# Two transformer layers on one core: the wait for the end of a GpSimd call at every third call instead of every second, and the engines' order chosen anew

## The reference

```
x = x + 0.5 * moe_swiglu(ln(x))          # f = 0
x = x + rwkv_time_mixing(ln(x))          # f = 1: a scan along the sequence
x = x + 0.5 * moe_swiglu(ln(x))          # f = 2, same weights as f = 0
x = x + 0.5 * moe_silu(ln(x))            # f = 3
x = x + retention(ln(x))                 # f = 4: 16 heads of 8, decay mask, group norm
x = x + 0.5 * moe_silu(ln(x))            # f = 5, same weights as f = 3
```

## Time and profile before

| what | value |
|---|---|
| median of 3 runs | 724.55 us (722.36 to 731.54) |
| profiled execution, its own time | 730.31 us |
| its span | 728.4 us |
| mean granted TensorE clock | 0.94 |
| busy: TensorE, VectorE, ScalarE, GpSimd | 606.1, 386.8, 344.1, 399.4 us |

### The profile page before, as it was taken

One profiled execution on the slowest core, in us unless ns is written; L12 is line 12 of the kernel. 1 busy time (PEld: TensorE's weight loads), 2 busy tenths in 40 slices (PEclk: granted clock), 3 DMA queues, 4 the chain that ended last, 5 costly groups with the idle time before them and its releaser, 6 DMA issues.

```text
span 728.4 us, 13112 instructions
## 1 busy us (share of the span) xinstructions
PE 606.1 (83%) x4180; PEld 513.3 (70%) x4180; DVE 386.8 (53%) x1056; ACT 344.1 (47%) x667; POOL 399.4 (55%) x400
## 2 busy tenths in 40 slices
PE   3398998999598886888789988999678989996891
PEld 2388977678576875878778878656644659886881
DVE  6513416797679753533162206797777985500005
ACT  2355556755367534653366567314233124653450
POOL 2556756674457645655556666632205764566662
PEclk9999999999699989997999999999969999999996
DMA  8345213112311223221142213100211111211314
GB/s 335 125 135 199 41 38 102 40 38 59 95 34 30 59 49 99 73 45 33 41 105 67 45 52 96 40 19 12 81 29 23 30 29 29 66 43 44 91 45 145
DMA packets 45121, 50.21 MB, mean 69 GB/s; under 512 B 14456, under 2 KB 36344, under 8 KB 45056
## 3 DMA queue, kind: packets, MB, share of 16 engines
q0 software_dynamic: 11776, 24.14, 13.5%
q1 hardware_dynamic: 31904, 24.44, 10.6%
q10 hardware_dynamic: 1376, 0.79, 0.4%
HBM read 32.04 MB, written 17.29 MB: 68 GB/s over the span
## 4 chain that ended last, share of the span: by engine, by line
PE 63%; DVE 10%; DMA 9%; issue 8%; ACT 5%; POOL 4%; ACTq 1%; POOLq 0%; DVEq 0%
PE bank L621 18%; PE bank L601 14%; PE bank L608 10%; DMA xs<-tokens_in,idx_in 6%; PE pair L709 5%; PE pair L741 3%; PE bank L582 2%; POOL xs L1101 2%; PE pair L545 2%; PE pair L525 2%; DMA tokens_out<-ys,idx_out 2%; POOL tokens_out L1113 1%; ACT w_up L840 1%; ACT hT L861 1%; ACT ys L908 1%
## 5 line engine op out<-in xcount | busy, mean ns | idle before, releaser
L1113 POOL DMA_INDIRECT tokens_out<-ys,idx_out x184 | 195.1, 1060 | 158.4 <-ACT ys L908 80.5
L1101 POOL DMA_INDIRECT xs<-tokens_in,idx_in x184 | 193.7, 1053 | 147.1 <-DVE owner L1261 36.6
L621 PE MATMUL bank<-w,hT 128*128 x1288 | 184.5, 288 | 22.7 <-ACT ys L908 10.4
L621 PEld LDWEIGHTS bank<-w,hT 128*128 128x128 f32 x1288 | 166.6, 199 | 41.1 <-issue 39.9
L601 PE MATMUL bank<-xT_kept,w_up 128*128 128x128 f32 x1104 | 163.2, 297 | 17.6 <-ACT gate L858 6.9
L601 PEld LDWEIGHTS bank<-xT_kept,w_up 128*128 128x128 f32 x1104 | 149.2, 209 | 31.8 <-issue 17.8
L840 ACT ACTIVATE w_up<-w 128x728 f32 (+1 forms) x184 | 128.9, 718 | 47.1 <-PE bank L608 17.3
L1281 DVE TENSOR_TENSOR hT<-gate,bank 128x384 f32<-128x384 f32 x92 | 50.5, 549 | 121.8 <-PE bank L601 60.8
L608 PE MATMUL bank<-xT_kept,w_up 128*128 128x128 f32 x736 | 101.6, 286 | 10.0 <-ACT hT L861 7.3
L608 PEld LDWEIGHTS bank<-xT_kept,w_up 128*128 128x128 f32 x736 | 92.4, 197 | 20.0 <-issue 11.9
L908 ACT ACTIVATE ys<-bank 128x256 f32<-128x256 f32 x96 | 35.9, 374 | 103.0 <-PE bank L621 52.6
(11 more groups left out here) (169 smaller groups left out, 639.6 us busy)
## 6 DMA issues: line engine op xcount, KB each, us to landing
yg<-tokens_out SPq DMA_DIRECT2D x60, 128.0 KB, 3.0
w<-in_w SPq DMA_DIRECT2D x8, 536.0 KB, 8.3
w<-in_w SPq DMA_DIRECT2D x8, 512.0 KB, 5.3
xs<-tokens_in,idx_in POOLq DMA_INDIRECT x184, 2.8
tokens_out<-ys,idx_out POOLq DMA_INDIRECT x184
tokens_in<-xn SPq DMA_DIRECT2D x8, 256.0 KB, 7.1
tokens_in<-xn SPq DMA_DIRECT2D x8, 254.0 KB, 2.5
sq<-in_square SPq DMA_DIRECT2D x1, 768.0 KB, 13.2
```

The source lines that it names most:

```text
L621: last = mm(y, hT[0:n_f, n % 2, c * P:(c + 1) * P], w_of(k, e, WD[k] + c * P, P, n_f), start=(c == 0), stop=(k == 0 and c == CH[k] - 1))
L1101: pool.indirect_dma_start(xs[:, j % RING, :], None, xn_dram[KIND[f]][b], tile_rows(idx_in, b, j), engine_sem=described)\
L1113: pool.indirect_dma_start(ys_dram[b], tile_rows(idx_out, b, j), ys[:, j % RING, :], None, engine_sem=described)\
```

## The change

BURST becomes 3, so the wait for the end of the calls before stands at every third call instead of every second. All five strings of TURNS are new. No instruction is added or removed but the waits: of the 368 calls (numbered from 0), 183 had the wait before (2, 4, ... 366), and 122 have it now (3, 6, ... 366). The programs themselves are the same. A line or two of the table stand for the rest:

```diff
@@ -42,7 +42,7 @@
 RING = 8
-BURST = 2
+BURST = 3
 ROUND23 = 65536.0
@@ -91,41 +91,41 @@
...
     "pool":
-        "b c b h2 a2 c6 f d c2 e c a c7 e c e a e2 c3 e c e3 c a e2 d2 c e d2 e5 g e7 d9 f2 d3 f d3 f2 d f4 d f d f2 d "
-        "f11 c8 e2 c4 e c e c4 e c2 e c e c2 e4 c e9 d4 e2 d e d9 f d f d2 f2 d f d f d2 f3 d2 f4 c3 f c f c f3 c4 f5 "
...
+        "h a b2 c h a c6 e c6 e c e c e c e c d a e c e c2 e c2 e2 c e c d e2 a e2 a e d e d e d e2 f e4 d4 f2 d7 f3 d6 "
+        "f2 d f5 d f11 c11 e c3 e2 c g c e c2 e c2 e c2 e2 c e12 d5 e3 d10 f d4 f2 d f2 d2 f7 d f2 c3 f c f2 c f c3 f5 "
...
```

## The result

On one chip the changed kernel took 700.06 us in the median (696.13 to 700.92, 4 runs) and the kernel before 727.03 us (722.36 to 731.54, 4 runs): ratio 0.9617, interval 0.9579 to 0.9656, so 3.8% faster. On another chip the changed kernel came out at 0.9621 again.

The account below looks back on a forecast made before the run. GpSimd, the second full engine after TensorE, was taken to bound six windows. 12.3 us (pace) + 4.2 (order) - 0.6 (VectorE) = 15.9 at most; half, 8 us, took the median from 724.55 to 716.5 us, range 706 to 729.

Parts of the forecast that it names:

- The wait's price: GpSimd's calls: an end wait costs 0.45 us as second wait; 61 waits removed give back 27.4 us.
- the windows: Six stretches between gathers landing just as TensorE wanted them; only GpSimd time there was to count.
- the choice of 164 calls: GpSimd's calls inside the six windows, taken as the path; at 0.075 us each, 12.3 us.
- The 0.6 us for calls that VectorE holds up: About 8 GpSimd calls from 212 to 248.5 us gain nothing beside VectorE: 0.6 us less.
- The halving: Half of the 15.9 us ceiling taken, 8 us, since slack and other waits would absorb part.
- The pace: GpSimd's spacing per call falls from 1.485 to 1.41 us, at most 12.3 us in the six windows.
- some 2 us of work lost: Clock drop behind TensorE's wait at 665.70: 6.5 us at 1.2 GHz; a removed gap may spare it.
- the second rival: TensorE takes the whole 15.9 us and two or three clock drops don't happen: 704 to 710 us, chance 0.17.
- 3 x 1.41 = 4.2 us: New order moves the gather at 247.81 from call 125 to 122, 4.2 us earlier on top of the pace.
- The pace is off the path: Rival: TensorE and hand-offs to ScalarE set the end, GpSimd only becomes idle: 721 to 727 us, chance 0.27.
- Scatters hold up gathers: Rival: last pass's last gather, now six scatters later, stalls TensorE; two or three such places: 728 to 742 us, chance 0.11.
- The third call isn't cheap: Rival: a third GpSimd call without a wait is held as long as with it: 724 to 732 us, chance 0.05.

Follow-up runs that it names:

- E10: Kernel before, all 183 end waits kept, written first in the 101 calls outside the six windows and second inside: 728.43 us, ratio 1.0003.
- E5: Kernel before, all 183 end waits kept at every second call, but written ahead of the other wait: 714.1 us, ratio 0.9807.
- E1: Kernel before with its old order, the end wait at every third call instead of every second: 713.19 us, ratio 0.9789.
- E2: Kernel before with only the new order of steps, the end wait still at every second call: 716.11 us, ratio 0.9826.
- E13: Old order, end wait at every third call, one gather moved from call 125 to 122: 792.70 us, ratio 1.0679.
- E9: Kernel before, all 183 end waits kept, written first in the 82 calls inside the six windows and second elsewhere: 713.08 us, ratio 0.9789.
- E4: Changed kernel with the end wait at every fourth call instead of every third: 697.23 us, ratio 0.9555.
- E6: Changed kernel's new order with an end wait at every call, written ahead of the other waits: 696.0 us, ratio 0.9559.

## Why the prediction was wrong

**What held.** The spacing (1.25, 1.26, 1.74 us), GpSimd's busy time, the third call without a wait being cheap, TensorE's wait for gathers at 12.1 us, no rise of its waits for ScalarE in sum. The wait's price held as well: some 55 to 61 fewer calls have the 0.75 us, 25 to 27 us against the 27.4 expected. (That the idle time before the calls fell by 32.0 us is no test of it: with the pace alone it fell by 11.7.) Nothing outside the windows counted (E10), so the choice of 164 calls was right. Only its cause was put loosely: not that a call has two waits, but that the end wait is written behind the other (E5). The 0.6 us for calls that VectorE holds up was not measured by itself. In the trace before, the 162 calls with no VectorE work beside them took 1.06 us at most, and all 22 calls over 1.5 us had some beside them, which is how the row of 3.08 us was read.

**The halving, first failed step.** The pace was to give 12.3 us at most and was taken at half, since "inside the windows the groups between the edges had slack". E1 gave 14.5 us in the medians, 15 by the ratio (12.5 at least by its interval): all of the 12.3, and more. The remark behind the halving, that TensorE has only 11.5 us of waits on paced gathers to lose, was the misleading bound. That wait did fall by no more than about 8 us (19.4 to 11.2 in E1), but TensorE's busy time fell by 10.3 us with it (606.1 to 595.8). 7 of these are the clock: it was busy at the lower level for 48.1 us instead of 62.5. What the other 3 are isn't shown. The prediction had the mechanism, priced at "some 2 us of work lost" for a drop, and then put it on the other side of a scale instead of adding it. This was the second rival, given 0.17, though its range of 704 to 710 doesn't reach the measured 700.06 either. ("Full pace from edge to edge" was read from the last two windows only. In the longest, 332.70 to 404.30, GpSimd is busy for 42.68 of 71.6 us, 0.60 where full pace is 0.65, so there was some slack, and the time from pass 5 to 6 still became 4 us shorter in E1.)

**The order, second failed step, and the larger one.** It was priced by the one gather that the chain of waits ran through: "3 x 1.41 = 4.2 us". Measured alone it is worth 12.7 us (E2). The term stood at the wrong place. That gather did come early, and much more so than predicted:

```profile
227.05 0.98 POOL L1101 DMA_INDIRECT xs<-tokens_in,idx_in  x1 [0.31 <-issue]
```

It was at 247.81 and was expected at 242. It is 20.8 us earlier, but the next pass starts only 11.3 us earlier (256.30 for 267.64), of which 8.8 had been won by the start of its own pass (177.78 for 186.55). So 12 us at the gather on the chain were worth 2.5 us at the next pass, and the pace alone gives those 2.5 without moving it (81.0 to 78.6 us in E1, 78.5 in the changed kernel). The term of 4.2 us measured nothing. (The run that moved this gather alone, E13, is not usable, so this rests on the traces of single executions.) What the order won lay elsewhere: before the second pass, in the stretch behind it, and from pass 6 to 7, where it took 30 matmuls out of the way. It came as 24.6 us less of TensorE's busy time at the lower clock in E2, and as waits for VectorE that are gone. The chain of waits named TensorE for 63% and the prediction never asked in which order TensorE took its own steps. Four of the five strings that changed were left unpriced.

**The rivals.** "The pace is off the path" is refuted by E1, and E9 shows its true half: it becomes so once the windows are served. "Scatters hold up gathers" did not happen, though the last gather is call 355: it was issued at 665.31, and from 640 us on no transpose waited for a gather. The new order does cost 2.5 us in the last pass all the same, against the pace alone (88.7 for 86.2 us); by what, no run shows. "The third call isn't cheap" is refuted by the timeline. No rival's range holds the measured time: both terms of the sum were too small at once, and no rival had the order worth more than 4.2 us.

**The sum, after the fact.** The pace 12.3 us and some 3 for the clock, the order 12.7: 28 us off 728, or 700. The 12.7 is what E2 measured. No way to work it out from the trace before was shown.

## What to carry to other kernels

Where every call of an engine has two waits, look in the timeline at the idle time by the order in which the waits are written, before thinning them out: here the same wait written first cost nothing, and that kernel is, with E4, the fastest of all (0.9546 and 0.9555). Price a new order on each engine whose string changed, stretch by stretch, by TensorE's busy time, its clock and the matmuls that it has to do there; the one link on the chain that this order moved was worth nothing measurable. Where an engine at full pace stands between two tight edges, take its time in full as long as the step is small (12 us here; 37 gave no more), and add what the clock gives back.

## What the runs showed of the hardware that was not expected

A wait of GpSimd for the end of its own call before cost 0 or 0.45 us by its place alone: idle 0.75 us in the earlier trace rows, 0.30 in E5 and E6 with the same releaser. Freeing 37 us of GpSimd's time in the tight windows gave no more than freeing 12 (E9, E1). And a kernel's time can move by 11% with stalls in several engines that have no releaser in the trace (E13: 792.7 us; E1, one gather away: 713.2), which a ratio to the kernel before does not take out. Making one indirect DMA took 0.94 to 1.06 us when VectorE did nothing beside it (162 calls before) and up to 3.08 us beside VectorE's operations on 128x1024 elements.
